# Mixture of experts: routing weights reach the hidden rows by copies within SBUF instead of by products with a selector table

## The chip, the cores and the metric

The kernel runs on one core of one Trainium2 chip. The metric is device time in microseconds (us): the median of three runs of the kernel before is 797.15 us (796.9 to 798.04).

## The reference

The program is one pass over 1024 tokens (4 sequences of 256) of width 256, in float32, through two layers: attention with a memory branch, a gated feed-forward net, a second feed-forward block, latent attention with 16 heads, and last a mixture of experts. The change is in that last part:

```python
h = layernorm(x)                      # 1024 x 256
p = softmax(h @ gate_w.T)             # 16 experts
w, idx = top_k(p, 6)                  # six experts of each token, not normalised again
for e in range(16):                   # experts of 176 hidden columns
    g, u = split(h @ w1[e].T)
    y += c[:, e] * ((silu(g) * u) @ w2[e].T)   # c[t, e] = p[t, e] if e is chosen, else 0
y += shared expert (352 hidden columns, no weight)
out = x + y
```

A routing weight is a number for each token and expert. The kernel multiplies it into the hidden values, before the second product.

## The kernel before, in words

The program has five instruction streams: TensorE (PE) for products, ScalarE (ACT), VectorE (DVE), GpSimd (POOL), and SyncE (SP), which only starts transfers (DMAs). The function `plan()` writes one list of items. Each engine goes through that list in order and runs the items it has a part in, so order on an engine is the order of the list. Engines wait for each other by semaphores: `mark` counts one up, `at` is the value to wait for.

**Tiling of the mixture.** The hidden columns of the shared expert (352, padded to 384) and of the 16 experts (16 x 176 = 2816) stand side by side and are cut into 25 blocks of 128, named moe0 to moe24: 3 of the shared expert and 22 with routing weights, which are here called the gated ones. As 176 is no multiple of 128, a gated block often holds rows of two experts. Tokens are cut into two halves of 512. One unit of work is `(j, half)`, with the 128 hidden rows of block j on the partitions and 512 tokens along them. Products are made in three parts (high times high, high times low, low times high), since a float32 value is split in two fp32r values.

- `step("moe", j, half)`: PE makes 12 products of 512 columns, which fill two PSUM banks (g and u). ACT takes silu of g (L1017). DVE multiplies with u (L1368). For a gated unit DVE then multiplies with the routing weights (L1375). ACT copies the result to the high part VVh (L1024), and DVE subtracts to get the low part VVl (L1380), which sets `th`.
- `down("moe", j, half)`: PE waits for `th` and adds the block into the sums with 12 products of 256 columns (all of these at L555).

The list interleaves them. With lag 3, group m of the list is (m, half 0) and then (m-3, half 1), and each `down` comes one `step` later. On PE a group therefore reads: step (m, 0), down (m-4, 1), step (m-3, 1), down (m, 0), and then step (m+1, 0), down (m-3, 1) of the next one. There are four PSUM banks for all steps, used in turn.

**Weights.** A block's weights (384 KB) are loaded by SP into one of three raw buffers `wr`, split by POOL into a high and a low part (L1665, L1667; `split`), and used by PE. There are six slots for split parts, so POOL splits block m+2 when down (m-4, 1) is done, in group m. The raw buffer that this frees takes block m+5:

```python
before = CHUNKS[i - NRAW][0]          # NRAW = 3: the block three before this one
...
e.wait_ge(*at("part", before))        # SP waits until POOL has split it
```

**Routing weights before.** `route` computes `cl`, 128 tokens x 16 weights, and on DVE splits it in high and low, 32 columns in all. `spread(half)` turns it on PE (L874), and ACT copies it to `CTr[0:32, 512 tokens of the half]` (L1126). A table `SELr` (32 x 2816, zeros and ones) is loaded as `SELf` and rounded by POOL in the item `selector` (L1706, L1708, L1710). In every gated step PE makes one product more, `SELr` block times `CTr` (L691), into a PSUM bank of its own. DVE reads the weights there.

**Queues around the change.** SP's stream is, for the whole stage, only the loads of blocks, each behind its wait, and at the end the stores. POOL's is splits and a few small operations.

Of the kernel before, what the change touches and what calls it, by code (L numbers as in the profile page):

```python
# [143 lines left out]
def plan():  # L144
# [5 lines left out]
    def item(*a):  # L150
        order.append(a)
# [194 lines left out]
    split(9)  # L346
    item("selector")

# [18 lines left out]
def program(nc, outer, S, B, x, w, sm, sel, out):  # L367
    mark, at, now = S.mark, S.at, S.now

    def sb(name, shape, dt=F32, ctx=outer):  # L370
        return ctx.enter_context(nc.sbuf_tensor(name, shape, dt))
# [92 lines left out]
    VV = [(sb(f"VVh{i}", [128, 512], R32, ctx=m1), sb(f"VVl{i}", [128, 512], R32, ctx=m1)) for i in range(3)]  # L464
    SELf = sb("SELf", [32, 22 * 128], ctx=m1)
    SELr = sb("SELr", [128, 22 * 128], R32, ctx=m1)
    CTr = sb("CTr", [128, T], R32, ctx=m1)
# [11 lines left out]
    def bank(*key):  # L479
        return banks[B.of(*key)]  # L480
# [60 lines left out]
    def tensor(x):  # L541
# [132 lines left out]
        def step(run, j, half):  # L674
            name = f"{run}{j}"
            hi, lo = parts[PART[name]]
            xin, turned = {"mem": (AT, "tq"), "ffn": (BT, "tf"), "moe": (AT, "te")}[run]
            sl = half_cols(half)
            e.wait_ge(*at("part", name))
            e.wait_ge(*vacated(turned, half, 1))  # L680
            for part in range(2 if RUN[run][1] else 1):
                b = fills(ring["w"], "gu"[part], run, j, half)
                o = part * 256
                mm3(b[:, :], [((hi[:, o + k * 128:o + k * 128 + 128], lo[:, o + k * 128:o + k * 128 + 128]),
                               (xin[0][:, k, sl], xin[1][:, k, sl])) for k in range(2)]).then_inc(
                    *filled("gu"[part], run, j, half))
            if run == "moe" and j >= 3:
                b = fills(ring["w"], "c", run, j, half)
                e.wait_ge(*at("selr"))
                e.wait_ge(*vacated("sp", half))  # L690
                x.matmul(b[:, :], SELr[:, (j - 3) * 128:(j - 2) * 128], CTr[:, sl], start=True, stop=True).then_inc(  # L691
                    *filled("c", run, j, half))

# [176 lines left out]
        def spread(half):  # L870
            b = fills(ring["w"], "sp", half)
            e.wait_ge(*at("rt", half))
            for c in range(4):
                p = x.transpose(b[0:32, c * 128:(c + 1) * 128], cl[:, half * 4 + c, :], ident)  # L874
            p.then_inc(*filled("sp", half))
# [34 lines left out]
    def scalar(x):  # L910
# [212 lines left out]
        def spread(half):  # L1123
            e.wait_ge(*at("blank"))
            e.wait_ge(*have("sp", half))
            x.copy(CTr[0:32, half_cols(half)], bank("sp", half)[0:32, :]).then_inc(*vacates("sp", half))  # L1126

# [13 lines left out]
    def vector(x):  # L1141
# [209 lines left out]
        def step(run, j, half):  # L1351
# [10 lines left out]
            if run == "mem":  # L1362
                x.scalar_tensor_tensor(out=b[:, :], in0=a[:, :], scalar=1.0, in1=a[:, :], op0=ALU.add,
                                       op1=ALU.mult).then_inc(*mark("hid", run, j, half))
                S.same(("t1", k), ("hid", run, j, half))
            else:
                e.wait_ge(*have("u", run, j, half))
                x.tensor_tensor(b[:, :], a[:, :], bank("u", run, j, half)[:, :], ALU.mult).then_inc(  # L1368
                    *vacates("u", run, j, half))
                S.value["t1", k] = vacated("u", run, j, half)  # L1370
                S.same(("hid", run, j, half), ("t1", k))
                if run == "moe" and j >= 3:
                    e.wait_ge(*have("c", run, j, half))
                    e.wait_ge(*vacated("u", run, j, half))
                    x.tensor_tensor(b[:, :], b[:, :], bank("c", run, j, half)[:, :], ALU.mult).then_inc(  # L1375
                        *vacates("c", run, j, half))
                    S.value["hid", run, j, half] = vacated("c", run, j, half)
            hh, hl = (VV if run == "moe" else HH)[c]
# [186 lines left out]
        def route(half):  # L1565
# [19 lines left out]
            x.scalar_tensor_tensor(out=cl[:, hs, 16:32], in0=rp[:, hs, 0:16], scalar=0.0, in1=pr[:, hs, 0:16],  # L1585
                                   op0=ALU.is_lt, op1=ALU.mult).then_inc(*mark("dv"))
            e.wait_ge(*now("dv"))
            x.tensor_copy(chr_[:, hs, :], cl[:, hs, 16:32]).then_inc(*mark("dv"))
            e.wait_ge(*now("dv"))
            x.tensor_copy(cl[:, hs, 0:16], chr_[:, hs, :].bitcast(F32)).then_inc(*mark("dv"))  # L1590
            e.wait_ge(*now("dv"))
            x.tensor_tensor(cl[:, hs, 16:32], cl[:, hs, 16:32], chr_[:, hs, :].bitcast(F32), ALU.subtract).then_inc(
                *mark("rt", half))

# [14 lines left out]
    def gpsimd(x):  # L1609
# [92 lines left out]

        def selector():
            for s in latent_end():
                e.wait_ge(*s)
            x.memset(CTr[:, :].bitcast(F32), 0.0).then_inc(*mark("blank"))  # L1706
            e.wait_ge(*at("sel"))
            x.memset(SELr[:, :].bitcast(F32), 0.0).then_inc(*mark("selz"))  # L1708
            e.wait_ge(*at("selz"))
            x.tensor_scalar(SELr[0:32, :], SELf[:, :], 1.0, 0.0, ALU.mult, ALU.add).then_inc(*mark("selr"))  # L1710

        run(order, {"norm1": norm1, "rotate": rotate, "mask": mask, "l0begin": l0begin, "split": split, "memnorm": memnorm,
                    "memturn": memturn, "ffnmean": ffnmean, "expert": expert, "latstd": latstd, "l1norm": l1norm,
                    "endnorm": endnorm, "selector": selector})

    def sync(x_):
# [3 lines left out]
        def load(name):  # L1720
            i = INDEX[name]
            if i >= NRAW:
# [16 lines left out]
        for name, _, _ in CHUNKS[NRAW:]:  # L1739
            if name == "moe5":  # L1740
                for s in latent_end():
                    e.wait_ge(*s)
                x_.dma_start(SELf[:, :], sel).then_inc(*mark("sel", by=16))
            load(name)
        for t in range(NT):
            e.wait_ge(*at("st", t))
            x_.dma_start(ov[:, t, :], XO[:, t, :]).then_inc(*mark("out", t, by=16))
# [121 lines left out]
```

## Time and profile before

| what | value |
|---|---|
| median of three runs | 797.15 us |
| profiled execution: its time | 799.59 us |
| its span, first to last instruction | 797.8 us |
| mean granted TensorE clock | 0.948 |
| busy PE, DVE, ACT, POOL | 703.8, 469.2, 324.4, 248.0 us |
| DMA queue q1, share of 16 engines | 10.9% |

The profile is of one execution. A row of the timeline gives the start and duration of an instruction and in brackets how long its engine had been idle and what released it. PE's products overlap: one product of 512 columns is shown as 0.39 us long, but the next starts 0.23 us after it, so starts have to be subtracted to get what one costs. PEclk is the granted clock as a share of 2.4 GHz; 0.50 is 1.2 GHz. The mixture stage goes from about 553 us to the end.

### The profile page before, as it was taken

Reading aid. Unit: us, or ns where it says so; the run is one execution under the profiler, and the core shown is the slowest. Engines: PE = TensorE matmul, PEld = TensorE weight load, DVE = VectorE, ACT = ScalarE, POOL = GpSimd, SP = SyncE. Lnnn points to the kernel's source line nnn. Section 1 sums busy time; section 2 is a strip of 40 time slices with the busy share of each in tenths; the row PEclk is TensorE's granted clock in tenths of the full one; section 3 lists DMA queues with packets and bytes.
Section 4 is the critical chain, followed back from the end, with each engine's and each line's share of the span. In section 5 each row is a group of like instructions: output and inputs, shape, how many; then the busy total and the mean of one; then the engine's idle time right before and its main releaser. Section 6 shows DMA issues by size and latency. Waiting matters only on the chain.

```text
span 797.8 us, 11864 instructions
## 1 busy us (share of the span) xinstructions
PE 703.8 (88%) x4468; PEld 580.5 (73%) x4468; DVE 469.2 (59%) x1058; ACT 324.4 (41%) x773; POOL 248.0 (31%) x330
## 2 busy tenths in 40 slices
PE   4986599999888699867799998988599999999997
PEld 2764378788777588756677776766488888888886
DVE  4789777776437686564565546473654444444444
ACT  2424144554533233323676674664232222222221
POOL 1236510100324722314434432343423334333400
PEclk9989699999999799979899998999799999999999
DMA  6323000000112100000100000001111111111001
GB/s 215 100 66 97 14 1 1 2 1 1 47 37 63 44 18 21 1 20 24 38 1 2 2 1 1 1 2 39 39 28 53 41 40 40 51 48 41 1 1 53
DMA packets 11672, 25.82 MB, mean 32 GB/s; under 512 B 1344, under 2 KB 3392, under 8 KB 11584
## 3 DMA queue, kind: packets, MB, share of 16 engines
q1 hardware_dynamic: 11616, 25.07, 10.9%
q8 instruction: 35, 0.57, 0.3%
q14 instruction: 21, 0.17, 0.1%
HBM read 24.02 MB, written 1.05 MB: 31 GB/s over the span
## 4 chain that ended last, share of the span: by engine, by line
PE 71%; DVE 17%; ACT 5%; issue 4%; POOL 1%; DMA 1%; SPq 0%; DVEq 0%; ACTq 0%; POOLq 0%
PE ps L555 45%; PE ps L650 4%; PE ps L621 4%; PE ps L838 3%; PE ps L633 3%; PE ps L826 3%; PE ps L816 2%; DVE NB L1172 1%; PE ps L563 1%; ACT AO L1107 1%; PE ps L691 1%; PE ps L624 1%; PE ps L577 1%; DVE sml L1513 1%; ACT PB L1095 1%
## 5 line engine op out<-in xcount | busy, mean ns | idle before, releaser
L1696 POOL TENSOR_SCALAR PB<-PB,sml 128x256 f32<-128x256 f32 x128 | 59.1, 483 | 96.9 <-DVE sml L1530 96.9
L1024 ACT CAST VVh<-U 128x512 fp32r<-128x512 f32 x50 | 31.0, 620 | 128.0 <-PE ps L555 99.9
L1368 DVE TENSOR_TENSOR U<-U,ps 128x512 f32<-128x512 f32 x50 | 34.3, 687 | 73.9 <-PE ps L555 73.9
L555 PE MATMUL ps<-ATh,wh 128*128 128x512 f32 x176 | 72.5, 412 | 5.4 <-POOL wl L1667 2.5
L555 PE MATMUL ps<-ATh,wl 128*128 128x512 f32 x176 | 71.2, 405 | 0.0
L555 PE MATMUL ps<-ATl,wh 128*128 128x512 f32 x176 | 71.1, 404 | 0.0
L1665 POOL TENSOR_SCALAR wh<-wr 128x768 fp32r<-128x768 f32 (+3 forms) x31 | 24.1, 777 | 140.6 <-PE ps L555 140.4
L1095 ACT ACTIVATE PB<-ps,sml 128x256 f32<-128x256 f32 x128 | 59.5, 492 | 12.7 <-DVE sml L1524 12.7
L1380 DVE TENSOR_TENSOR VVl<-U,VVh 128x512 fp32r<-128x512 f32 x50 | 40.5, 811 | 36.9 <-ACT VVh L1024 36.9
L650 PEld LDWEIGHTS ps<-VK,PT 128*128 128x128 f32 x384 | 49.3, 191 | 12.0 <-issue 11.4
L1667 POOL TENSOR_TENSOR wl<-wr,wh 128x768 fp32r<-128x768 f32 (+3 forms) x31 | 55.6, 1793 | 2.6
L1107 ACT COPY AO<-ps 128x512 f32<-128x512 f32 x64 | 35.2, 589 | 48.6 <-PE ps L826 48.4
L985 ACT ACTIVATE P<-SS 128x384 f32<-128x384 f32 (+1 forms) x48 | 26.8, 558 | 57.8 <-DVE SS L1323 57.8
L555 PE MATMUL ps<-wh,VVh 128*128 128x256 f32 x136 | 39.3, 289 | 11.7 <-DVE VVl L1380 11.7
L650 PE MATMUL ps<-VK,PT 128*128 128x33 f32 x384 | 46.8, 267 | 0.0
L826 PE MATMUL ps<-SM,PB 128*128 128x128 f32 x256 | 36.8, 286 | 10.2 <-POOL PB L1696 5.2
L1017 ACT ACTIVATE U<-ps 128x512 f32<-128x512 f32 x50 | 29.9, 599 | 38.0 <-PE ps L555 38.0
L1319 DVE TENSOR_REDUCE mx<-ps 128x2 f32<-128x384 f32 (+1 forms) x48 | 28.8, 599 | 26.4 <-PE ps L624 26.3
L621 PE MATMUL ps<-KB,QKT 128*128 128x384 f32 (+1 forms) x96 | 43.5, 535 | 0.0
L555 PEld LDWEIGHTS ps<-ATh,wh 128*128 128x128 f32 x176 | 34.1, 194 | 12.8 <-POOL wl L1667 2.7
L838 PE MATMUL ps<-AO,X 128*64 128x256 f32 x256 | 34.8, 393 | 7.8 <-DVE UTl L1534 7.7
L1513 DVE TENSOR_REDUCE sml<-ps 128x2 f32<-128x512 f32 x64 | 40.9, 680 | 0.0
(257 smaller groups left out, 2051.7 us busy)
## 6 DMA issues: line engine op xcount, KB each, us to landing
wr<-in_w SPq DMA_DIRECT2D x32, 384.0 KB, 3.1
wr<-in_w SPq DMA_DIRECT2D x16, 321.0 KB, 3.0
wr<-in_w SPq DMA_DIRECT2D x11, 256.0 KB, 2.6
XO<-in_x SPq DMA_DIRECT2D x2, 512.0 KB, 4.7
out_dram<-XO SPq DMA_DIRECT2D x8, 128.0 KB, 1.7
wr<-in_w SPq DMA_DIRECT2D x2, 416.0 KB, 6.1
AO<-in_sm SPq DMA_DIRECT2D x1, 448.0 KB, 7.3
SELf<-in_sel SPq DMA_DIRECT2D x1, 352.0 KB, 3.9
```

The source lines that it names most:

```text
L555: t = x.matmul(o, a, b, start=first and i == 0 and c == 0, stop=last and i == n - 1 and c == 2, skip_group_check=skip)
L621: x.matmul(bk[:, 0:n], QKT[:, g, b * 256 + qt * 128:b * 256 + qt * 128 + 128], KB[u % 2][:, h0:h0 + nh, cols], start=True, stop=False)
L650: p = x.matmul(o, pt[:, c * 128:(c + 1) * 128], vk4[:, t - qt + k, 8 * g + h, :], start=k == 0, stop=k == qt)
L826: p = x.transpose(bk[:, kc * 256 + qt * 128:kc * 256 + qt * 128 + 128], PB[i % 3][:, 2 * i2 + qt, kc * 128:kc * 128 + 128], ident)
L838: p = x.matmul(bk[64 * i2:64 * i2 + 64, 0:256], CN[:, 2 * b + kc, :], PN[(2 * i + i2) % 4][:, kc * 256:kc * 256 + 256], start=kc == 0, sto ...
L1095: a = x.activation(p[:, c, :], v[:, qt, :], ACT.Exp, bias=m[:, 8 + c:9 + c], scale=SC, accum_out=m[:, 12 + c:13 + c])
L1107: x.copy(PN[k % 4], bank("lt", i, i2)[:, :]).then_inc(*vacates("lt", i, i2))
L1368: x.tensor_tensor(b[:, :], a[:, :], bank("u", run, j, half)[:, :], ALU.mult).then_inc(*vacates("u", run, j, half))
L1380: x.tensor_tensor(hl[:, :], b[:, :], hh[:, :].bitcast(F32), ALU.subtract).then_inc(*mark("th", run, j, half))
L1513: x.tensor_reduce(m[:, 2 * i2:2 * i2 + 2], bank("ls", i, i2)[:, :].rearrange("p (q k) -> p q k", q=2), AX_X, ALU.max).then_inc(*mark("dv"))
L1667: x.tensor_tensor(lo[:, 0:k], raw[:, 0:k], hi[:, 0:k].bitcast(F32), ALU.subtract).then_inc(*mark("part", name))
L1696: t = x.tensor_scalar(p[:, c, :], p[:, c, :], m[:, 16 + c:17 + c], 1.0, ALU.mult, ALU.mult)
```

## The change

The selector table, its load, POOL's `selector` item and the PE product at L691 are gone. `cl` keeps 16 columns of plain float32 (three small DVE operations of `route` are gone), and `CTr` is 16 x 1024. Six buffers `CB0` to `CB5` (128 x 512) are new. SP fills one of them for each gated unit by copies from `CTr`: a piece of a block that belongs to expert e copies row e of `CTr` (one partition, 512 tokens, 2 KB) to all partitions of the piece. 8 of the 22 blocks lie in one expert and need one copy, 14 need two, so the 44 units take 72 copies of 256 KB per unit. DVE multiplies from `CB` in SBUF.

```diff
-            if run == "moe" and j >= 3:
-                b = fills(ring["w"], "c", run, j, half)
-                e.wait_ge(*at("selr"))
-                e.wait_ge(*vacated("sp", half))
-                x.matmul(b[:, :], SELr[:, (j - 3) * 128:(j - 2) * 128], CTr[:, sl], start=True, stop=True).then_inc(
-                    *filled("c", run, j, half))
...
                 if run == "moe" and j >= 3:
-                    e.wait_ge(*have("c", run, j, half))
+                    k = gated.index((j, half))
+                    e.wait_ge(*at(f"spread{k % NSPREAD}", k))
                     e.wait_ge(*vacated("u", run, j, half))
-                    x.tensor_tensor(b[:, :], b[:, :], bank("c", run, j, half)[:, :], ALU.mult).then_inc(
+                    x.tensor_tensor(b[:, :], b[:, :], CB[k % NSPREAD][:, :], ALU.mult).then_inc(*mark("gated", k))
...
-        def selector():
-            x.memset(CTr[:, :].bitcast(F32), 0.0).then_inc(*mark("blank"))
-            x.memset(SELr[:, :].bitcast(F32), 0.0).then_inc(*mark("selz"))
-            x.tensor_scalar(SELr[0:32, :], SELf[:, :], 1.0, 0.0, ALU.mult, ALU.add).then_inc(*mark("selr"))
...
+        def spread():
+            k = sent[0]
+            j, half = gated[k]
+            sent[0] += 1
+            e.wait_ge(*vacated("sp", half))
+            if k >= NSPREAD:
+                e.wait_ge(*at("gated", k - NSPREAD))
+            first = (j - 3) * 128
+            for x0 in range(first // 176, (first + 127) // 176 + 1):
+                a, b = max(x0 * 176, first) - first, min(x0 * 176 + 176, first + 128) - first
+                src = bass.AP(CTr, x0 * T + half * 512, [[T, 1], [0, b - a], [1, 512]])
+                x_.dma_start(CB[k % NSPREAD][a:b, :], src).then_inc(
+                    *mark(f"spread{k % NSPREAD}", k, by=16))
...
         for name, _, _ in CHUNKS[NRAW:]:
-            if name == "moe5":
-                x_.dma_start(SELf[:, :], sel).then_inc(*mark("sel", by=16))
+            if name.startswith("moe"):
+                while sent[0] < len(gated) and gated[sent[0]][0] + 3 * gated[sent[0]][1] <= int(name[3:]) - 6:
+                    spread()
             load(name)
+        while sent[0] < len(gated):
+            spread()
```

`j + 3 * half` is the number m of the group a unit is in. So the copies of group m stand on SP between the load of block m+5 and the load of block m+6; those of groups 19 to 24 and of the last three units stand behind the last load.

SP's stream before, from the load of moe4 (`wr0`) to that of moe10; `s_part` is POOL's split of the block three before:

```order
47 L1730 DMA wr0<-in_w 128x768 [waits s_part]
48 L1743 DMA SELf<-in_sel 32x2816 [waits s_x3,s_pn2,s_hi,s_full7]
49 L1730 DMA wr1<-in_w 128x768 [waits s_part]
50 L1730 DMA wr2<-in_w 128x768 [waits s_part]
51 L1730 DMA wr0<-in_w 128x768 [waits s_part]
52 L1730 DMA wr1<-in_w 128x768 [waits s_part]
53 L1730 DMA wr2<-in_w 128x768 [waits s_part]
54 L1730 DMA wr0<-in_w 128x768 [waits s_part]
```

SP's stream now, from the load of moe8 to that of moe12; `CB0` is for unit (3, 0), `CB1` for (4, 0), `CB2` for (5, 0), `CB3` for (6, 0) and `CB4` for (3, 1):

```order
51 L1709 DMA wr1<-in_w 128x768 [waits s_part]
52 L1726 DMA CB0<-CTr 128x1x512 [waits s_free4]
53 L1709 DMA wr2<-in_w 128x768 [waits s_part]
54 L1726 DMA CB1<-CTr 48x1x512
55 L1726 DMA CB1<-CTr 80x1x512
56 L1709 DMA wr0<-in_w 128x768 [waits s_part]
57 L1726 DMA CB2<-CTr 96x1x512
58 L1726 DMA CB2<-CTr 32x1x512
59 L1709 DMA wr1<-in_w 128x768 [waits s_part]
60 L1726 DMA CB3<-CTr 128x1x512
61 L1726 DMA CB4<-CTr 128x1x512 [waits s_free6]
62 L1709 DMA wr2<-in_w 128x768 [waits s_part]
```

The copies moved in between the loads; a copy for group m follows the load that waits for POOL's split of block m+2.

POOL's stream before, from the split of moe3 (`yh`) to that of moe5 (`wh`):

```order
182 L1665 TENSOR_SCALAR yh<-wr 128x768 [waits s_x3,s_hi,s_pn2,s_full7,s_raw2]
183 L1667 TENSOR_TENSOR yl<-wr,yh 128x768 [waits s_part_hi]
184 L1665 TENSOR_SCALAR yh<-wr 128x768 [waits s_raw0]
185 L1667 TENSOR_TENSOR yl<-wr,yh 128x768 [waits s_part_hi]
186 L1706 MEMSET CTr 128x1024
187 L1708 MEMSET SELr 128x2816 [waits s_sel]
188 L1710 TENSOR_SCALAR SELr<-SELf 32x2816 [waits s_selz]
189 L1665 TENSOR_SCALAR wh<-wr 128x768 [waits s_full4,s_raw1]
190 L1667 TENSOR_TENSOR wl<-wr,wh 128x768 [waits s_part_hi]
```

POOL's stream now, over the same splits:

```order
182 L1653 TENSOR_SCALAR yh<-wr 128x768 [waits s_x3,s_hi,s_pn2,s_full7,s_raw2]
183 L1655 TENSOR_TENSOR yl<-wr,yh 128x768 [waits s_part_hi]
184 L1653 TENSOR_SCALAR yh<-wr 128x768 [waits s_raw0]
185 L1655 TENSOR_TENSOR yl<-wr,yh 128x768 [waits s_part_hi]
186 L1653 TENSOR_SCALAR wh<-wr 128x768 [waits s_full7,s_raw1]
187 L1655 TENSOR_TENSOR wl<-wr,wh 128x768 [waits s_part_hi]
```

The three selector operations are gone, and nothing takes their place.

## Rows read from the trace of the kernel before

**Rows 1.** The page: busy time by engine, and the first lines of the chain

```profile
PE 703.8 (88%) x4468; PEld 580.5 (73%) x4468; DVE 469.2 (59%) x1058; ACT 324.4 (41%) x773; POOL 248.0 (31%) x330
...
PE ps L555 45%; PE ps L650 4%; PE ps L621 4%; PE ps L838 3%; PE ps L633 3%; PE ps L826 3%; PE ps L816 2%; DVE NB L1172 1%; PE ps L563 1%; ACT AO L1107 1%; PE ps L691 1%; PE ps L624 1%; PE ps L577 1%; DVE sml L1513 1%; ACT PB L1095 1%
```

**Rows 2.** Windows, core 0: us, busy (x) by engine, PEclk, DMA share, GB/s

```profile
600.00:640.00 40.00, 40.00 (x226) 34.68 (x226) 18.08 (x26) 10.98 (x18) 12.62 (x9) 1.00 0.14 41
```

**Rows 3.** Timeline in mid stage: start us, us, engine line op [idle before <-releaser]

```profile
656.28 0.69 DVE L1375 TENSOR_TENSOR U<-U,ps 128x512 f32<-128x512 f32 x1
...
656.89 0.40 PE L555 MATMUL ps<-ATh,wh 128*128 128x512 f32 x1
...
657.21 0.83 POOL L1665 TENSOR_SCALAR wh<-wr 128x768 fp32r<-128x768 f32 x1 [5.85 <-PE ps L555]
...
658.13 2.16 POOL L1667 TENSOR_TENSOR wl<-wr,wh 128x768 fp32r<-128x768 f32 x1
...
659.68 0.39 PE L691 MATMUL ps<-CTr,SELr 128*128 128x512 f32 x1
...
659.92 0.28 PE L555 MATMUL ps<-wh,VVh 128*128 128x256 f32 x1
...
660.32 0.33 SPq L1730 DMA_DIRECT2D wr<-in_w  x1
...
660.75 0.69 DVE L1375 TENSOR_TENSOR U<-U,ps 128x512 f32<-128x512 f32 x1
...
661.35 0.40 PE L555 MATMUL ps<-ATh,wh 128*128 128x512 f32 x1
...
661.52 0.62 ACT L1024 CAST VVh<-U 128x512 fp32r<-128x512 f32 x1 [2.44 <-PE ps L555]
...
662.18 0.69 DVE L1380 TENSOR_TENSOR VVl<-U,VVh 128x512 fp32r<-128x512 f32 x1 [0.74 <-ACT VVh L1024]
...
666.15 0.83 POOL L1665 TENSOR_SCALAR wh<-wr 128x768 fp32r<-128x768 f32 x1 [5.86 <-PE ps L555]
```

**Rows 4.** The selector product: xcount, ns min/median/max, first and last start

```profile
L691 PE MATMUL ps<-CTr,SELr x44: 392/393/397, 578.9 to 789.1; 128*128 128x512 f32 x44
```

**Rows 5.** The normalisation's vector operation: ns min/median/max

```profile
L1172 DVE TENSOR_SCALAR NB<-XO,mv,rs x24: 398/407/5234, 310.4 to 559.3; 128x256 f32<-128x256 f32 x24
```

**Rows 6.** Timeline at the stage's start

```profile
559.28 1.80 POOL L1667 TENSOR_TENSOR yl<-wr,yh 128x768 fp32r<-128x768 f32 x1
...
561.91 2.44 POOL L1708 MEMSET SELr<- 128x2816 f32 x1
...
565.77 1.74 DVE L1380 TENSOR_TENSOR VVl<-U,VVh 128x512 fp32r<-128x512 f32 x1 [0.68 <-ACT VVh L1024]
...
567.57 0.58 PE L555 MATMUL ps<-wh,VVh 128*128 128x256 f32 x1 [10.29 <-DVE VVl L1380]
```

**Rows 7.** Windows on the granted clock

```profile
560.00:562.00 2.00, 0.00 (x0) 0.00 (x0) 2.00 (x1) 0.00 (x0) 2.00 (x3) 0.64 0.38 152
...
570.00:572.00 2.00, 2.00 (x12) 1.63 (x11) 0.00 (x0) 0.57 (x1) 0.00 (x0) 0.80 0.00 0
...
488.00:492.00 4.00, 1.47 (x8) 1.14 (x10) 3.44 (x10) 0.32 (x1) 0.46 (x1) 0.61 0.00 0
```

**Rows 8.** The page's DMA issues: weight load, KB each, us to landing

```profile
wr<-in_w SPq DMA_DIRECT2D x32, 384.0 KB, 3.1
```

**Rows 9.** Windows on DMA: last two numbers are busy share, GB/s

```profile
7.00:8.00 1.00, 0.00 (x0) 0.00 (x0) 0.72 (x5) 0.00 (x0) 0.60 (x1) 1.00 1.04 412
...
662.00:663.00 1.00, 1.00 (x6) 0.77 (x6) 0.69 (x1) 0.19 (x2) 0.00 (x0) 1.00 0.69 273
```

**Rows 10.** Timelines, POOL after the gate product and at moe6, DVE at the end

```profile
584.36 1.82 POOL L1667 TENSOR_TENSOR wl<-wr,wh 128x768 fp32r<-128x768 f32 x1
...
593.76 0.83 POOL L1665 TENSOR_SCALAR wh<-wr 128x768 fp32r<-128x768 f32 x1 [7.58 <-PE ps L555]
...
790.17 0.69 DVE L1375 TENSOR_TENSOR U<-U,ps 128x512 f32<-128x512 f32 x1
```

More of the change, by code:

```diff
@@ L22 @@
 LAG = 5
+NSPREAD = 6
 NEG = -1.0e30
@@ L346, in plan @@
     split(9)
-    item("selector")
     def moe_after(half):
@@ L440, in program @@
     nm = sb("nm", [128, 4, NT])
-    chr_ = sb("chr", [128, NT, 16], R32)
-    cl = sb("cl", [128, NT, 32])
+    cl = sb("cl", [128, NT, 16])
     ml = ExitStack()
@@ L464, in program @@
     VV = [(sb(f"VVh{i}", [128, 512], R32, ctx=m1), sb(f"VVl{i}", [128, 512], R32, ctx=m1)) for i in range(3)]
-    SELf = sb("SELf", [32, 22 * 128], ctx=m1)
-    SELr = sb("SELr", [128, 22 * 128], R32, ctx=m1)
-    CTr = sb("CTr", [128, T], R32, ctx=m1)
+    CTr = sb("CTr", [16, T], ctx=m1)
+    CB = [sb(f"CB{i}", [128, 512], ctx=m1) for i in range(NSPREAD)]
     parts += [(sb(f"yh{i}", [128, SLOT], R32, ctx=m1), sb(f"yl{i}", [128, SLOT], R32, ctx=m1)) for i in range(2)]
@@ L472, in program @@
     n_units = len(us)
+    gated = [tuple(o[2:]) for o in order if o[0] == "step" and o[1] == "moe" and o[2] >= 3]
     cb = small("cb")
@@ L873, in spread @@
             for c in range(4):
-                p = x.transpose(b[0:32, c * 128:(c + 1) * 128], cl[:, half * 4 + c, :], ident)
+                p = x.transpose(b[0:16, c * 128:(c + 1) * 128], cl[:, half * 4 + c, :], ident)
             p.then_inc(*filled("sp", half))
@@ L1123, in spread @@
         def spread(half):
-            e.wait_ge(*at("blank"))
+            if half == 0:
+                for s in latent_end():
+                    e.wait_ge(*s)
             e.wait_ge(*have("sp", half))
-            x.copy(CTr[0:32, half_cols(half)], bank("sp", half)[0:32, :]).then_inc(*vacates("sp", half))
+            x.copy(CTr[:, half_cols(half)], bank("sp", half)[0:16, :]).then_inc(*vacates("sp", half))
         run(order, {"norm1": norm1, "fuse": fuse, "turn1": turn1, "project": project, "headnorm": headnorm,
@@ L1372, in step @@
                 if run == "moe" and j >= 3:
-                    e.wait_ge(*have("c", run, j, half))
+                    k = gated.index((j, half))
+                    e.wait_ge(*at(f"spread{k % NSPREAD}", k))
                     e.wait_ge(*vacated("u", run, j, half))
-                    x.tensor_tensor(b[:, :], b[:, :], bank("c", run, j, half)[:, :], ALU.mult).then_inc(
-                        *vacates("c", run, j, half))
-                    S.value["hid", run, j, half] = vacated("c", run, j, half)
+                    x.tensor_tensor(b[:, :], b[:, :], CB[k % NSPREAD][:, :], ALU.mult).then_inc(*mark("gated", k))
+                    S.same(("hid", run, j, half), ("gated", k))
             hh, hl = (VV if run == "moe" else HH)[c]
@@ L1584, in route @@
             e.wait_ge(*now("dv"))
[L1585 to L1593, printed above, removed]
+            x.scalar_tensor_tensor(out=cl[:, hs, :], in0=rp[:, hs, 0:16], scalar=0.0, in1=pr[:, hs, 0:16], op0=ALU.is_lt,
+                                   op1=ALU.mult).then_inc(*mark("rt", half))
         def store(t):
@@ L1701, in endnorm @@
             rsqrt(rs, ve, half, "ve4", "rs4")
-        def selector():
-            for s in latent_end():
-                e.wait_ge(*s)
-            x.memset(CTr[:, :].bitcast(F32), 0.0).then_inc(*mark("blank"))
-            e.wait_ge(*at("sel"))
-            x.memset(SELr[:, :].bitcast(F32), 0.0).then_inc(*mark("selz"))
-            e.wait_ge(*at("selz"))
-            x.tensor_scalar(SELr[0:32, :], SELf[:, :], 1.0, 0.0, ALU.mult, ALU.add).then_inc(*mark("selr"))
         run(order, {"norm1": norm1, "rotate": rotate, "mask": mask, "l0begin": l0begin, "split": split, "memnorm": memnorm,
                     "memturn": memturn, "ffnmean": ffnmean, "expert": expert, "latstd": latstd, "l1norm": l1norm,
-                    "endnorm": endnorm, "selector": selector})
+                    "endnorm": endnorm})
     def sync(x_):
@@ L1731, in load @@
                 *mark(f"raw{i % NRAW}", name, by=16))
+        sent = [0]
+        def spread():
[11 more added lines that the diff above has]
+                    *mark(f"spread{k % NSPREAD}", k, by=16))
         x_.dma_start(XO[:, 0:4, :], xv[:, 0:4, :]).then_inc(*mark("xin0", by=16))
@@ L1739, in sync @@
         for name, _, _ in CHUNKS[NRAW:]:
-            if name == "moe5":
-                for s in latent_end():
-                    e.wait_ge(*s)
-                x_.dma_start(SELf[:, :], sel).then_inc(*mark("sel", by=16))
+            if name.startswith("moe"):
+                while sent[0] < len(gated) and gated[sent[0]][0] + 3 * gated[sent[0]][1] <= int(name[3:]) - 6:
+                    spread()
             load(name)
+        while sent[0] < len(gated):
+            spread()
         for t in range(NT):
```

## The prediction

> **What bounds the kernel now.** I read the page's busy times first, then the chain, then the mixture stage in windows and as a timeline. On the page PE is busy 88% of the span, and nearly half of the chain that ended last is line L555, the three-part products [rows 1]. In the middle of the stage the window shows 40.00 of 40.00 us busy at a granted clock of 1.00, while DVE has 18 us of work and the DMA engines are 14% busy [rows 2]. So here each product taken from PE is time, and transfers are idle capacity. Whether that capacity can be used depends on when a copy starts and how long it takes.
>
> The timeline gives the beat [rows 3]. A step's 12 products start at 656.89, and the next thing behind them, the selector product, starts at 659.68: a step costs 2.79 us. The selector product costs 0.24 us (659.68 to 659.92) and a down 1.43 us (659.92 to 661.35). POOL begins one split at 657.21 and the next at 666.15, so a group of two units takes 8.94 us. The order within a group matters most. I call t0 the moment when down (m-4, 1) is over and step (m-3, 1) begins: 656.89. DVE had multiplied routing weights into unit (m, 0) at 656.28, 0.6 us before t0. POOL's split of block m+2 runs from 657.21 to 660.29, and SP issues the load of block m+5 at 660.32, t0 + 3.4.
>
> **What goes.** 44 selector products [rows 4] at 0.24 us: 10.6 us, all of it on PE's path as long as PE is the bound.
>
> POOL's three selector operations go too, and they cost something where one would not look. The first down waits for a DVE operation and begins at 567.57 after 10.29 us of idle PE [rows 6]. DVE was late because the last normalisation before it took 5.23 us where 0.41 us is usual [rows 5]; it began at 559.3 and ended when POOL's memset of `SELr` (561.91 for 2.44 us) did. The VVl operation then took 1.74 us against 0.69 elsewhere [rows 6, 3], beside POOL's last selector operation. Without them DVE's wait ends with POOL's last split at 561.1, normalisation ends at about 561.5, and the first down begins 4.0 us earlier. (561.5 + 0.7 for the product with silu + 0.7 for ACT + 0.7 for VVl = 563.6; such operations take 0.69 and 0.62 us in [rows 3].) I take off 4.0 us; the bounds are 0 and 5. The three DVE operations gone from `route` work on 64 columns and are hidden behind PE, as is the smaller copy to `CTr`: nothing. The multiplication from `CB` has the shape of L1380, 0.69 us, like the one from PSUM: nothing either.
>
> **What comes: the start of a copy.** SP takes its stream in order. Copies of group m stand behind the load of block m+5, which is issued at t0 + 3.4. But DVE wants the copy of unit (m, 0) at t0 - 0.6. So even a copy that took no time would be 4 us late, and behind it on DVE stand its VVl, the whole next unit (m-3, 1), and so down (m, 0) on PE with everything after it. This does not heal: the next load waits for a split that waits for down (m-3, 1), which waits for this copy. The late copy is inside the loop that sets the period. It holds for m = 4 to 19. From there on no load stands ahead, and six copies can be in flight.
>
> **What comes: how long a copy takes.** The load of 384 KB lands 3.1 us after its issue [rows 8], and the copies queue behind it. No row shows a copy out of one partition, so I bound it.
> - Low end: 256 KB at the rate of all engines. In the window after that load they moved 273 GB/s [rows 9]: 0.96 us; I take 0.9.
> - High end: all 16 engines read one and the same 2 KB row. The best that rows show for one engine, which fills one partition's row at a time, is 412 GB/s over 16 engines [rows 9], 25.7 GB/s each. That is also the best that they show for one partition. 262,144 bytes at it are 10.2 us. It could be slower still; no row bounds it.
>
> I take 10 us. Every copy of this change has a single partition as its source, and the nearest row for what one partition gives is the 25.7 GB/s; 273 GB/s is a rate over many partitions.
>
> The Trainium skill, page "SBUF — State Buffer", section "Door 1: The DMA port swizzle (why [64,N] ≈ [32,N])", says that a transfer's rate depends on how many of 16 ports its partitions reach, and gives 27.6 GB/s for partitions 0 to 3, which share one port. By that figure a copy takes 9.5 us, and the sum below would be 22 us less. No run so far shows it for reads.
>
> **The clock.** At the stage's start PE fell idle at 557.3 and the granted clock dropped to 1.2 GHz in the window 560 to 562; it was back near 570.8 [rows 7], 3.2 us after PE had begun again, which costs 1.6 us of work. The window at 488 shows the same with PE idle for about 2.5 of 4 us. Pauses of 5 us and more in each group should do it each time: 1.6 us per group, bounds 0 and 1.6.
>
> **The sum, for a copy of 10 us.** After a copy lands: 2.2 us until VVl is ready (660.75 to 662.87 in [rows 3], and a wake-up).
> - Unit (3, 0): its copy stands behind the load of moe8, which waits for POOL's split of moe5; that ends at 586.2 [rows 10], now 582.2. Landing at 582.2 + 3.1 + 10 = 595.3; VVl 597.5; down, step, down (5.6) and clock (1.6): t0 of group 4 is 604.7. It was 593.4 its row in [rows 10], less 0.3.
> - Groups 4 and 5 have one copy each: 3.4 + 3.1 + 10 + 2.2 + 5.6 + 1.6 = 25.9 us. Twice: 656.5.
> - Groups 6 to 18 have two, and the second ends last: 3.4 + 3.1 + 20 + 2.2 + 1.4 for down (m-3, 1), at half clock 1.4 more = 31.5 us. 13 of them: 1066.0.
> - The last 15 units' copies follow one another: 3.4 + 3.1 + 150 = 156.5: 1222.5.
> - From the last weighted multiplication to the end of the span it was 797.8 - 790.17 [rows 10] = 7.6 us, with clock 9: span 1231.5.
> The profiled execution's own time was 1.8 us above its span, and 2.4 us above the median of the runs: 1231 us, rounded to 1230. The 10.6 us are in this sum only in that the selector product isn't in a period; PE is no longer the bound.
>
> **Rivals.**
> - *Copies run at the rate of all engines.* For: the queue is nearly empty, and 16 engines each have 8 rows to write. Against: one row as source. A period is then 3.4 + 3.1 + 0.9 + 2.2 + 5.6 + 1.6 = 16.8 us. Unit (3, 0) gives t0 = 582.2 + 3.1 + 0.9 + 2.2 + 5.6 + 1.6 = 595.6; 16 groups (4 to 19): 864.4. The rest was 797.8 - (593.4 + 16 x 8.94) = 61.4, less 12 selector products (2.9): span 922.9, time 922. Without the clock's part 896.
> - *The row serves a few engines at once.* With 5 us a copy, a group takes 3.4 + 3.1 + 5 + 2.2 + 5.6 + 1.6 = 20.9 us, the last 15 copies 81.5 us: 599.7 + 15 x 20.9 + 81.5 + 9 = 1003.7, about 1003.
> - *Slower than one engine's best rate.* 14 us a copy: 44 x 4 = 176 more, 1406.
> - *On the other side: copies are in time, and the kernel is faster.* 799.6 - 10.6 - 4.0 - 2.4 = 782.6. It needs every copy to have landed 0.6 us before t0, that is, to be issued some 5 us before t0 instead of 3.4 us after. That would be so if the load before it did not wait for POOL's split of block m+2, because POOL had run ahead. Against: POOL's rows show it idle 5.86 us before each split and released by PE; SP follows it within 0.03 us [rows 3]. It is decided by the order of SP's stream, which is as printed.
>
> **How the numbers follow.** A copy of 9.5 to 11 us: 0.55. All engines' rate: 0.25. Between: 0.08. Slower than 11 us: 0.07. In time: 0.04. The last 0.01 is for something that makes no difference. The likeliest one's own range is 1195 to 1265: 44 x 0.5 us below, 15 x 1.6 for the clock where pauses cost less, and 0.8 us a copy above. The range for 8 in 10 has to reach down to the case of quick copies without the clock's cost, 895. Beyond about 0.2% either way a run of this kernel can be told from no change: faster 0.04, same 0.01, slower 0.95.
>
> **What would show it.** In the profile after, L691 is gone, and the first down's wait is some 4 us shorter. DVE's multiplication from `CB` is released by a DMA, in each group up to 19. Copies at one row's rate: the DMA share goes near 1 while GB/s is near 26, a copy lands 10 us and the second 20 us after the load, and PE is busy about a third of a group. Copies at full rate: share low, and a period of 15 to 17 us. The granted clock falls in each group's pause. I am wrong in the mechanism if the copies' waits on DVE are short in groups 4 to 19, or if PE stays above 90% busy there.

## The result

The changed kernel takes 1144.18 us (median of 4 runs, 1141.88 to 1145.46); the kernel before took 797.6 us on the same chip (median of four runs; the 797.15 us above is that of three). The ratio is 1.4334, 95% interval 1.4295 to 1.4374: 347 us slower. The forecast was 1230 us with a range of 895 to 1265. The time lies in the range, and the direction and both reasons (copies start late, and each is limited by its source) held. It lies below the 1195 to 1265 that I gave as the likeliest case's own range: the cost of a pair of copies was too high. It is inside the stated range only because that range also reaches down to another case, that of quick copies.

### The profile page after: what moved, and what is told of

The parts are those of the page before. It is cut to its first block, busy times and chain, and to the rows that moved or that the text cites. A ratio compares the mean times of both kernels' runs of the same rounds, so it can differ in the third digit from the quotient of the medians.

```text
span 1143.7 us, 11867 instructions
## 1 busy us (share of the span) xinstructions
PE 755.6 (66%) x4416; PEld 616.1 (54%) x4424; DVE 456.4 (40%) x1052; ACT 319.9 (28%) x773; POOL 236.1 (21%) x327
## 4 chain that ended last, share of the span: by engine, by line
PE 37%; DMA 31%; DVE 13%; SPq 5%; POOL 5%; ACT 5%; issue 4%; DVEq 0%; ACTq 0%; POOLq 0%
DMA CB<-CTr 31%; PE ps L554 20%; SPq L1726 4%; PE ps L649 3%; PE ps L620 3%; PE ps L831 2%; POOL wl L1655 2%; PE ps L819 2%; PE ps L632 2%; PE ps L809 1%; DVE U L1371 1%; DVE VVl L1375 1%; ACT AO L1100 1%; ACT VVh L1017 1%; POOL wh L1653 1%
## 5 line engine op out<-in xcount | busy, mean ns | idle before, releaser
L1371 DVE TENSOR_TENSOR U<-U,CB 128x512 f32<-128x512 f32 x44 | 31.4, 713 | 415.6 <-DMA CB<-CTr 415.6
L554 PE MATMUL ps<-wh,VVh 128*128 128x256 f32 x136 | 52.3, 385 | 194.6 <-DVE VVl L1375 194.6
L554 PEld LDWEIGHTS ps<-wh,VVh 128*128 128x128 f32 x136 | 35.6, 262 | 206.6 <-DVE VVl L1375 206.3
L554 PE MATMUL ps<-yh,VVh 128*128 128x256 f32 x64 | 24.9, 390 | 112.2 <-DVE VVl L1375 112.2
L554 PE MATMUL ps<-ATh,wh 128*128 128x512 f32 x176 | 79.0, 449 | 5.4 <-POOL wl L1655 2.5
L554 PEld LDWEIGHTS ps<-yh,VVh 128*128 128x128 f32 x64 | 16.6, 259 | 119.1 <-DVE VVl L1375 119.1
L1375 DVE TENSOR_TENSOR VVl<-U,VVh 128x512 fp32r<-128x512 f32 x50 | 34.6, 692 | 37.4 <-ACT VVh L1017 37.4
L554 PE MATMUL ps<-wh,VVl 128*128 128x256 f32 x136 | 48.8, 359 | 0.0
L554 PE MATMUL ps<-wl,VVh 128*128 128x256 f32 x136 | 48.6, 357 | 0.0
L554 PEld LDWEIGHTS ps<-ATh,wh 128*128 128x128 f32 x176 | 39.2, 223 | 13.9 <-POOL wl L1655 2.7
L819 PE MATMUL ps<-SM,PB 128*128 128x128 f32 x256 | 36.8, 286 | 10.1 <-POOL PB L1684 5.1
## 6 DMA issues: line engine op xcount, KB each, us to landing
CB<-CTr SPq DMA_DIRECT2D x16, 256.0 KB, 17.4
CB<-CTr SPq DMA_DIRECT2D x8, 160.0 KB, 14.4
```

Of the source, the lines that this page charges most:

```text
L554: t = x.matmul(o, a, b, start=first and i == 0 and c == 0, stop=last and i == n - 1 and c == 2, skip_group_check=skip)
L819: p = x.transpose(bk[:, kc * 256 + qt * 128:kc * 256 + qt * 128 + 128], PB[i % 3][:, 2 * i2 + qt, kc * 128:kc * 128 + 128], ident)
L1371: x.tensor_tensor(b[:, :], b[:, :], CB[k % NSPREAD][:, :], ALU.mult).then_inc(*mark("gated", k))
L1375: x.tensor_tensor(hl[:, :], b[:, :], hh[:, :].bitcast(F32), ALU.subtract).then_inc(*mark("th", run, j, half))
```

## The profile after

The page of the changed kernel: busy time by engine, the costliest lines of the chain, the weighted multiplication with what it waited for, and the copy of 256 KB with its size and us to landing.

```profile
PE 755.6 (66%) x4416; PEld 616.1 (54%) x4424; DVE 456.4 (40%) x1052; ACT 319.9 (28%) x773; POOL 236.1 (21%) x327
...
DMA CB<-CTr 31%; PE ps L554 20%; SPq L1726 4%; PE ps L649 3%; PE ps L620 3%; PE ps L831 2%; POOL wl L1655 2%; PE ps L819 2%; PE ps L632 2%; PE ps L809 1%; DVE U L1371 1%; DVE VVl L1375 1%; ACT AO L1100 1%; ACT VVh L1017 1%; POOL wh L1653 1%
...
L1371 DVE TENSOR_TENSOR U<-U,CB 128x512 f32<-128x512 f32 x44 | 31.4, 713 | 415.6 <-DMA CB<-CTr 415.6
...
CB<-CTr SPq DMA_DIRECT2D x16, 256.0 KB, 17.4
```

Against [rows 1], PE's share fell from 88% to 66%, and a transfer now heads the chain: 31% of the span. Line L1371, the weighted multiplication, waited 415.6 us for copies, all 44 times. L691 is gone. The 17.4 us to landing is not one copy's price; it holds the time that a copy queues behind another.

The timeline of group 6, which answers to [rows 3] (start us, us, engine line, in brackets the idle time before and its releaser).

```profile
654.00 0.83 POOL L1653 TENSOR_SCALAR wh<-wr 128x768 fp32r<-128x768 f32 x1 [21.35 <-PE ps L554]
...
654.92 1.84 POOL L1655 TENSOR_TENSOR wl<-wr,wh 128x768 fp32r<-128x768 f32 x1
...
656.78 0.33 SPq L1709 DMA_DIRECT2D wr<-in_w  x1
657.16 1.15 SPq L1726 DMA_DIRECT2D CB<-CTr  x2
669.39 0.69 DVE L1371 TENSOR_TENSOR U<-U,CB 128x512 f32<-128x512 f32 x1 [16.18 <-DMA CB<-CTr]
...
678.32 0.69 DVE L1371 TENSOR_TENSOR U<-U,CB 128x512 f32<-128x512 f32 x1 [6.20 <-DMA CB<-CTr]
...
683.58 0.83 POOL L1653 TENSOR_SCALAR yh<-wr 128x768 fp32r<-128x768 f32 x1 [26.83 <-PE ps L554]
```

POOL begins the split at 654.00, 0.3 us after t0, SP issues the load at 656.78 and two copies right behind it. VectorE gets the first copy, for (6, 0), 12.6 us after the load's issue and the second, for (3, 1), 8.93 us later. The next split begins at 683.58. The group took 29.6 us where it took 8.94.

Two other pairs, in groups 9 and 11.

```profile
750.78 0.69 DVE L1371 TENSOR_TENSOR U<-U,CB 128x512 f32<-128x512 f32 x1 [15.79 <-DMA CB<-CTr]
...
758.12 0.69 DVE L1371 TENSOR_TENSOR U<-U,CB 128x512 f32<-128x512 f32 x1 [4.62 <-DMA CB<-CTr]
...
803.11 0.69 DVE L1371 TENSOR_TENSOR U<-U,CB 128x512 f32<-128x512 f32 x1 [16.34 <-DMA CB<-CTr]
...
807.52 0.69 DVE L1371 TENSOR_TENSOR U<-U,CB 128x512 f32<-128x512 f32 x1 [1.69 <-DMA CB<-CTr]
```

Here the second copy comes only 7.3 and 4.4 us after the first, with as many bytes. The difference is in whose rows they read. I call partitions 0 to 3, 4 to 7 and so on a four; expert e lies on partition e. In group 6 it is experts 2 and 0, on partitions 2 and 0. In group 9 it is experts 4 and 5, then 2. In group 11 it is 5 and 6, then 3 and 4. The number of transfers is not the difference: of the six groups whose copies all read one four, three have two transfers (28.3 to 29.6 us) and three have four (28.4 to 29.3 us), and the other seven groups, with three or four, took 23.4 to 26.0 us.

Windows of the changed kernel: us, busy time of PE, PEld, DVE, ACT and POOL, PEclk, DMA share, GB/s. The first lies wholly within a copy from one row, the second has copies from two fours in the queue (experts 4 and 5, then 2), the third covers the last copies (experts 13 to 15), the last most of the stage.

```profile
660.00:668.00 8.00, 0.00 (x0) 0.00 (x0) 0.00 (x0) 0.00 (x0) 0.00 (x0) 0.50 0.90 27
744.00:750.00 6.00, 0.00 (x0) 0.00 (x0) 0.00 (x0) 0.00 (x0) 0.00 (x0) 0.50 0.86 33
1085.00:1125.00 40.00, 24.57 (x101) 20.04 (x99) 8.59 (x14) 4.46 (x8) 0.00 (x0) 0.83 0.91 28
600.00:1000.00 400.00, 172.12 (x734) 142.48 (x732) 59.72 (x104) 33.95 (x61) 40.11 (x30) 0.71 0.56 33
```

The 16 engines are busy for 90% on average and move 27 GB/s between them. Compare [rows 9]: 412 GB/s at a share of 1.04. So an engine that is shown busy here moves few bytes. 262,144 bytes at 27 GB/s are 9.7 us; from the spacing of copies out of one four (8.8 to 9.1 us for the second of a pair, up to 9.8 us behind the last load) the rate is 27 to 30 GB/s. PEclk is 0.50 in the pauses and 0.71 over the stage, where it was 1.00 [rows 2].

The start of the stage, for [rows 6].

```profile
555.38 5.55 DVE L1167 TENSOR_SCALAR NB<-XO,mv,rs 128x256 f32<-128x256 f32 x4 [1.14 <-POOL rs L1604]
...
562.96 0.58 PE L554 MATMUL ps<-wh,VVh 128*128 128x256 f32 x1 [5.97 <-DVE VVl L1375]
```

The four normalisation operations take 5.55 us in all and TensorE waits 5.97 us before the first down instead of 10.29: 4.3 us less, where I had said 4.0.

## The experiments

### Earlier, and another source: the two causes taken apart

Two edits, alone and together. The first moves the copies of group m two loads ahead:

```diff
-                while sent[0] < len(gated) and gated[sent[0]][0] + 3 * gated[sent[0]][1] <= int(name[3:]) - 6:
+                while sent[0] < len(gated) and gated[sent[0]][0] + 3 * gated[sent[0]][1] <= int(name[3:]) - 4:
```

The second stores each half of `CTr` once to a table `ct` (16 x 1024) in HBM and copies from there:

```diff
+            if half not in stored:
+                stored.add(half)
+                x_.dma_start(ct[:, half_cols(half)], CTr[:, half_cols(half)]).then_inc(*mark(f"ct{half}", by=16))
+            e.wait_ge(*at(f"ct{half}"))
...
-                src = bass.AP(CTr, x0 * T + half * 512, [[T, 1], [0, b - a], [1, 512]])
-                x_.dma_start(CB[k % NSPREAD][a:b, :], src)
+                row = ct[x0:x0 + 1, half_cols(half)].to_broadcast([b - a, 512])
+                x_.dma_start(CB[k % NSPREAD][a:b, :], row)
```

**Early, from SBUF.** 

> The changed kernel with one edit: the copies of group m stand on SyncE two loads earlier (in front of the load of block m+4), so they are issued about two groups before they are needed; the copies themselves are the same. Theory (late start and slow copy both count, the source partition's port limits a copy): being early takes the waits for the split, the load and the vector chain out of the period, but 44 copies still pass one after another at 8.9 us where they share a port: at most 44 x 8.9 = 392 us from about 568, so an end near 970, and not under 860 if copies from different ports overlap as much as those of groups 8 to 19 did. Rival (only the place in SyncE's stream is wrong): every copy is in time and the result is 783 us.

Measured: 961.39 us (2 runs, ratio 1.2023, 1.1967 to 1.2079). From its list of waits (who waited for whom: us in total, times, longest):

```profile
DVE U L1371 <- DMA CB<-CTr: 228.8, 41, 7.4
```

Starting early gives back 183 us of the 347. What stays is the copies' own rate: VectorE still waits for 41 of 44. The bound of 970 was near: the multiplications came every 8.7 us on average. Overlap between fours saved little here: some copies came 4.7 to 7 us after the one before, but the last seven units all read experts 12 to 15, and most of those came 9.4 to 10.1 us apart.

**Late, from HBM.** 

> The changed kernel, with the copies in the same place, but their source is a table of 16 x 1024 weights in HBM, to which SyncE stores each half of CTr once (a small transfer and a wait for it, some 2 us, twice). Theory: a copy takes about 0.9 us behind the load, since no SBUF port is its bottleneck, and what is left is the late start: a period of 15 to 17 us in groups 4 to 19, 895 to 922 us in all. Rival 1 (late start costs nothing, only the slow copy does): about 785 us. Rival 2 (16 engines that read one row are slow wherever the row is): about 1144 us as with SBUF as the source.

Measured: 933.99 us (2 runs, ratio 1.1680, 1.1625 to 1.1736), 12 us above the stated span of cases. Its copies (KB each, us to landing) and group 8 on the timeline:

```profile
CB<-ct SPq DMA_DIRECT2D x16, 256.0 KB, 3.8
```

```profile
667.22 0.83 POOL L1653 TENSOR_SCALAR yh<-wr 128x768 fp32r<-128x768 f32 x1 [14.56 <-PE ps L554]
...
670.40 2.24 SPq L1731 DMA_DIRECT2D CB<-ct  x4
...
674.50 0.69 DVE L1371 TENSOR_TENSOR U<-U,CB 128x512 f32<-128x512 f32 x1 [8.07 <-DMA CB<-ct]
...
676.67 0.58 PE L554 MATMUL ps<-wh,VVh 128*128 128x256 f32 x1 [6.83 <-DVE VVl L1375]
...
677.32 0.69 DVE L1371 TENSOR_TENSOR U<-U,CB 128x512 f32<-128x512 f32 x1
```

A copy of 256 KB behind a load lands 3.8 us after its own issue (the median of 16). The second multiplication of the group follows without a wait. Even so VectorE waits 8.07 us for the first, and TensorE 6.83 us. The periods between splits are 16.7 to 17.7 us in mid stage, 17.1 on average, where my rival's sum had 16.8. Over 16 groups that is 5 of the 6.7 us by which the profiled span, 929.6, is above that sum's 922.9. So even a quick copy, started at t0 + 3.5, leaves the kernel 135 us above the one before (799.18 us in these runs): the late start alone is worse than the whole gain.

**Early, from HBM.** 

> Both: source in HBM, and the copies of group m in front of the load of block m+4. Theory: every copy is in time, TensorE is the bound again without the 44 selector products: 797.6 - 10.6 for these - 4 for the stage's start = 783 us, range 780 to 787. Rival: if the reading of one row stays slow in HBM, as in the run with the early copies from SBUF, far above 860.

Measured: 782.90 us (6 runs, 778.64 to 784.83, ratio 0.9776, 0.9742 to 0.9809). The window of mid stage:

```profile
640.00:740.00 100.00, 100.00 (x567) 86.89 (x566) 48.65 (x71) 29.28 (x48) 36.71 (x24) 1.00 0.35 108
```

TensorE is busy 100.00 of 100 us at full clock, as in [rows 2], and no multiplication waits for a copy. A unit's beat is 4.22 us, where it was 4.47 with the selector product: 0.24 us, times 44. With the 4 us at the start that is the 783 that was forecast. This is the version that beats both kernels, by 2.2% against before. The two causes can't be added up: one edit removes 183 us, the other 210, both 361, less than the sum of the two. The reason I give is that a slow copy hurts less when it has more time; no run shows that by itself.

### How early is early enough

One load earlier instead of two (`- 5` in place of `- 4`), from HBM.

> HBM as the source, and the copies of group m one load earlier than in the changed kernel (in front of the load of block m+5) instead of two. Theory: the copy of unit (m, 0) is then issued at 3.4 us after the t0 of group m-1, 8.5 us before that of group m, so 4.5 us before VectorE wants it; behind the load it lands 3.1 + 0.9 us later (3.8 to 4.1 in the run with late copies from HBM). It is in time by half a microsecond: 783 us, at most 790. Rival (the copies still sit in the loop that sets the period): a period above 8.5 us in groups 4 to 19, that is over 800 us.

Measured: 784.77 us (4 runs, ratio 0.9828, 0.9782 to 0.9874). Its timeline in group 7:

```profile
611.65 0.69 DVE L1371 TENSOR_TENSOR U<-U,CB 128x512 f32<-128x512 f32 x1 [0.27 <-DMA CB<-ct]
...
620.13 0.69 DVE L1371 TENSOR_TENSOR U<-U,CB 128x512 f32<-128x512 f32 x1 [0.30 <-DMA CB<-ct]
...
637.62 1.28 DVE L1371 TENSOR_TENSOR U<-U,CB 128x512 f32<-128x512 f32 x1 [0.88 <-DMA CB<-ct]
...
641.21 0.38 PE L554 MATMUL ps<-yh,VVh 128*128 128x256 f32 x1 [1.04 <-DVE VVl L1375]
```

Ten multiplications wait for their copy, 0.3 to 1.4 us, where theory had them half a microsecond early. TensorE does not feel eight of these waits. Behind the two longest, 0.88 us here and 1.44 us at 723.98, VVl comes to lie beside GpSimd's split and takes 1.5 us instead of 0.69, and TensorE waits 1.0 us each time. The margin worked out from t0 was thus right to about two microseconds, not to half of one. In time this run can't be told apart from the one with two loads (784.77 against 782.90, intervals 0.9782 to 0.9874 and 0.9742 to 0.9809). One load of distance is what separates 785 from 934.

### What limits a copy from SBUF: the row, or a port that rows share

**Experts four partitions apart.** `CTr` has 64 rows, expert e on row 4e. `cl` has 64 columns, of which every fourth is used and the rest are zeros:

```diff
-    CTr = sb("CTr", [16, T], ctx=m1)
+    CTr = sb("CTr", [64, T], ctx=m1)
...
-                p = x.transpose(b[0:16, c * 128:(c + 1) * 128], cl[:, half * 4 + c, :], ident)
+                p = x.transpose(b[0:64, c * 128:(c + 1) * 128], cl[:, half * 4 + c, :], ident)
...
-                src = bass.AP(CTr, x0 * T + half * 512, [[T, 1], [0, b - a], [1, 512]])
+                src = bass.AP(CTr, 4 * x0 * T + half * 512, [[T, 1], [0, b - a], [1, 512]])
```

> The changed kernel with expert e's weights on partition 4e of CTr instead of e (CTr has 64 rows, three of four are zeros and are not read); copies, their number and their place in SyncE's stream as in the changed kernel. Now neighbouring experts lie in different groups of four partitions. Theory (what limits a copy is a port that four neighbouring partitions share): blocks that belong to two experts, 28 of the 44 units, and pairs of copies that came from one group of four, pass in part side by side: each of these 28 units about 2.5 to 3 us quicker, 1045 to 1085 us in all. Rival (the limit is the single row that is read): the partition doesn't matter, 1144 us as before, within 10.

Measured: 1077.24 us (2 runs, ratio 1.3479, 1.3434 to 1.3524), inside the theory's span. The copy of 160 KB, always a neighbour of one of 96 KB, lands in 8.8 us, in the changed kernel in 14.4:

```profile
CB<-CTr SPq DMA_DIRECT2D x8, 160.0 KB, 8.8
```

```profile
CB<-CTr SPq DMA_DIRECT2D x8, 160.0 KB, 14.4
```

The copies, their number and their place are as they were; what has changed about them is the partition of their source. Two rows of one four don't pass side by side, two rows that lie four apart do in part. So the limit is not in the single row.

**The same weights on two partitions.** Each expert on e and on e + 32, and each piece in two halves; in the other run 64 stands in place of 32:

```diff
+                mid = (a + b) // 2
+                for lo, hi, r in ((a, mid, x0), (mid, b, x0 + 32)):
+                    src = bass.AP(CTr, r * T + half * 512, [[T, 1], [0, hi - lo], [1, 512]])
+                    x_.dma_start(CB[k % NSPREAD][lo:hi, :], src).then_inc(
```

> The changed kernel with the weights of each expert on two partitions, e and e + 32; each piece of a block is filled by two copies of half its rows, one from either partition. Theory (a port is shared by partitions, and e and e + 32 share one, by the Trainium skill, page 'SBUF — State Buffer', section 'Door 1: The DMA port swizzle (why [64,N] ≈ [32,N])'): no gain, 1144 us within 15. Rival (the limit is the single row): the two halves pass in part side by side, 3 us and more off each copy, about 1000 us.

> As the run with e and e + 32, but with e and e + 64, which by the same section lie on different ports. Theory: the halves pass in part side by side, as for unit (8, 0) of the changed kernel, whose two 64-row pieces come from experts 3 and 4: that copy had landed 9.2 us after the load's issue instead of 12.6. 3 to 3.7 us off each of 44 copies, 980 to 1020 us. Rival (something else than ports, e.g. the number of transfers): the same as with e + 32.

Measured: with + 32 1152.55 us (2 runs, ratio 1.4422, 1.4373 to 1.4470), with + 64 1033.01 us (2 runs, ratio 1.2926, 1.2882 to 1.2969). The first is within the 15 us that the theory allowed; what its 8 us above the changed kernel are made of was not taken apart. The two kernels have the same number of transfers in the same places. The load and VectorE's multiplications of group 6, first with + 32 and then with + 64:

```profile
658.47 0.33 SPq L1712 DMA_DIRECT2D wr<-in_w  x1
...
671.01 0.69 DVE L1371 TENSOR_TENSOR U<-U,CB 128x512 f32<-128x512 f32 x1 [16.11 <-DMA CB<-CTr]
...
679.96 0.69 DVE L1371 TENSOR_TENSOR U<-U,CB 128x512 f32<-128x512 f32 x1 [6.23 <-DMA CB<-CTr]
```

```profile
650.57 0.33 SPq L1712 DMA_DIRECT2D wr<-in_w  x1
...
661.25 0.69 DVE L1371 TENSOR_TENSOR U<-U,CB 128x512 f32<-128x512 f32 x1 [14.25 <-DMA CB<-CTr]
...
664.89 0.69 DVE L1371 TENSOR_TENSOR U<-U,CB 128x512 f32<-128x512 f32 x1 [0.92 <-DMA CB<-CTr]
```

With + 32 the second copy comes 8.95 us after the first, to 0.02 us what the changed kernel had. With + 64 it comes 3.64 us after. From the load's issue to the second multiplication it is 21.5 us with + 32 and 14.3 with + 64. This is what the Trainium skill says in "SBUF — State Buffer", section "Door 1: The DMA port swizzle (why [64,N] ≈ [32,N])": four neighbours and the four that are 32 away share one of 16 ports, those 64 away are on another. It gives 27.6 GB/s for one port, measured on transfers over partitions 0 to 3; here a single partition as source gave 27 in the windows, and up to 30 by the spacing of a pair. The runs agree with the page in the map, as far as it was tried (neighbours, + 4, + 32, + 64), and in the rate to about a tenth. The upper end of my forecast of 980 to 1020 for the second was 13 us too low: halves on two ports overlap, but not fully. Why not fully, no run shows.

### GpSimd's operations at the stage's start

The three selector operations put back into the early HBM version, on a tile that nothing reads:

```diff
+            x.memset(SELd[:, 0:1024], 0.0).then_inc(*mark("selz"))
+            e.wait_ge(*at("selz"))
+            x.memset(SELd[:, :], 0.0).then_inc(*mark("sely"))
+            e.wait_ge(*at("sely"))
+            x.tensor_scalar(SELd[0:32, :], SELd[0:32, :], 1.0, 0.0, ALU.mult, ALU.add)
```

> The run with HBM as the source and early copies, with GpSimd's three selector operations put back at their place (two memsets and one copy in the same sizes, on a tile that nothing reads). Theory (VectorE's normalisation is held up by GpSimd's memset at the stage's start, and TensorE waits for it): 4.0 us slower than without them, the first down begins 4 us later. Rival (GpSimd's operations are hidden): no difference, within 0.5 us.

Measured: 783.71 us (6 runs, ratio 0.9793, 0.9765 to 0.9820): not told apart from 782.90. The theory seemed to have failed. But the edit was not what the kernel before does. VectorE and GpSimd on the timeline:

```profile
551.49 6.44 DVE L1169 TENSOR_SCALAR NB<-XO,mv,rs 128x256 f32<-128x256 f32 x4 [1.14 <-POOL rs L1606]
...
556.84 0.95 POOL L1694 MEMSET SELd<- 128x1024 f32 x1
557.85 2.47 POOL L1696 MEMSET SELd<- 128x2816 f32 x1
557.86 0.67 DVE L1365 TENSOR_TENSOR U<-U,ps 128x512 f32<-128x512 f32 x1
...
559.21 0.69 DVE L1377 TENSOR_TENSOR VVl<-U,VVh 128x512 fp32r<-128x512 f32 x1 [0.68 <-ACT VVh L1019]
```

VectorE's normalisation ends after the short memset, and its next operation starts as the long one does. The wait that I had put between the two memsets left a gap in GpSimd's stream. In the kernel before there was none. Beside the long memset (557.85 to 560.32) VectorE then runs two operations of another kind, L1365 and L1377, in their usual 0.67 and 0.69 us. So it is not VectorE as a whole that a memset holds up, but this `tensor_scalar`. The second run has the first memset on a tile of its own and no wait behind it:

```diff
+            x.memset(SELc[:, :], 0.0).then_inc(*mark("selc"))
+            x.memset(SELd[:, :], 0.0).then_inc(*mark("selz"))
+            e.wait_ge(*at("selz"))
```

> HBM as source, early copies, and GpSimd's three selector operations put back, this time with no wait between the two memsets, as in the kernel before (in the first such run the wait between them let VectorE in). Theory (VectorE's last normalisation operation can't start until GpSimd's run of operations has a gap, so it ends with the long memset): TensorE's wait before the first down is 10.3 us again, 3.9 more than without them, and the time is 4 us above that of the run without them (782.9). Rival: as the first such run, under 1 us more.

Measured: 786.19 us (6 runs, ratio 0.9840, 0.9818 to 0.9862), 3.3 us above 782.90 by the medians.

```profile
556.42 8.82 DVE L1170 TENSOR_SCALAR NB<-XO,mv,rs 128x256 f32<-128x256 f32 x4 [1.14 <-POOL rs L1607]
...
561.76 0.95 POOL L1695 MEMSET SELc<- 128x1024 f32 x1
562.65 2.44 POOL L1696 MEMSET SELd<- 128x2816 f32 x1
565.17 0.67 DVE L1366 TENSOR_TENSOR U<-U,ps 128x512 f32<-128x512 f32 x1
```

TensorE's waits for VVl (total, times, longest), with the operations and without them:

```profile
PE ps L557 <- DVE VVl L1378: 12.0, 2, 10.3
```

```profile
PE ps L554 <- DVE VVl L1375: 7.6, 2, 6.0
```

Normalisation takes 8.82 us again, as in the kernel before, and ends with the long memset. TensorE's longest wait is 10.3 us against 6.0 without the operations, and 6.9 in the first run with the gap. The profile shows 4.3 us. The two runs' times, each with its own runs of before, differ by 3.3 us by the medians and by 5 us by the ratios, whose intervals do not meet. The theory holds, with the gap as its condition. The two runs with the operations also differ in the tile of the short memset; that this plays no part is assumed.

## Why the prediction was right, and where it was off

- **Removed, 44 x 0.24 us.** Right; seen where TensorE is the bound (beat 4.47 to 4.22 us). Worth nothing in the changed kernel.
- **The stage's start, 4.0 us.** Right in size (4.3) and cause, with a condition that I did not name: in the run with a gap between the memsets the normalisation got in there, so it is the unbroken run of GpSimd's operations that costs.
- **The late start of a copy.** Right. t0 of group 4 was forecast at 604.7 and came at 604.4, and t0 of group 6 at 656.5 against 653.7. Undoing only this took 183 us off, or 149 to 151 us where copies were quick.
- **10 us a copy.** Near: 12.6 us from the load's issue to the multiplication, where 13.1 was forecast. The choice of the single row's rate over that of all engines was right. The reading of it, "the best that they show for one partition", was not: the limit is a port that partitions share, which the three runs on placement showed. The 25.7 GB/s was one engine's share of a load; no run ties that to what a port gives a single row, so that the two figures lie close was luck.
- **The term that was too large: "Groups 6 to 18 have two, and the second ends last: 3.4 + 3.1 + 20 ...= 31.5 us".** It adds two copies end to end. Measured periods (starts of successive splits) are 28.3 to 29.6 us for the six groups whose copies all read one four (6, 7, 12, 13, 17, 18), mean 29.0, and 23.4 to 26.0 for the other seven, mean 25.3. 13 groups took 350.8 us instead of 409.5. That is 59 us of the error, of which a uniform 29.0 would have explained 33.
- **The last stretch** took 139 us from t0 of group 19 to the end instead of 165.5: 15 copies at 10 were forecast, and 4.9 to 9.8 us were measured. That is the other 26 us.
- **The clock.** It fell to 0.50 in the pauses of every group looked at, as said. No run took its cost apart; 1.6 us per group stays an estimate. In the late HBM run the periods agree with it to 1 us.
- **Two slips in the working.** The lower end of the likeliest case is 1230 less 22 less 24, which is 1184 and not 1195; the measured time lies below both. And the rival with 5 us a copy priced a group of two by its first copy (20.9 us); by the same sum its second copy ends last, at 21.5 us, and the rival's time is about 1011 us and not 1003.
- **The chances.** The rival "copies at the rate of all engines" had 0.25 and 922 us; the late HBM run shows it as a kernel of its own, at 934. The price of a copy fell in the case that had 0.55, but the time, 1144, lies where the working had only "between", at 0.08: between 922 and 1195.

## What to carry to other kernels

A transfer that replaces arithmetic has two prices, when its issue stands in its queue and what its source can give. Read both off the trace before counting the instructions saved: here one load of distance was worth 149 us with HBM as the source, and another source 210 us with the late start. A broadcast from one SBUF partition ran at 27 GB/s with all 16 engines taking part; from a small table in HBM it ran fast enough to be hidden. And if a copy stands behind a wait that its own result releases, its latency is paid in every turn of the loop.

## Not expected of the hardware

- The 16 DMA engines show 0.90 busy while they move 27 GB/s. The share of busy time says nothing of bytes here; share and GB/s have to be read together.
- SyncE is held up too: it issued a pair of SBUF copies in 1.1 to 1.2 us, but three or four of them in 5.8 to 8.3 us, where four from HBM took about 2 us. No run took apart what this costs.
- From HBM, 16 engines read one and the same 2 KB row without such a limit: 256 KB landed 3.8 us after issue, queued behind a 384 KB load.
- A gap between two GpSimd memsets was enough to let VectorE's waiting normalisation in: 6.44 us for its four operations with it, 8.82 us without, at the same work.
